# A graph-attention layer on one core: one head's max as relu(A*B - 1) on ScalarE into a PSUM bank, and the units' one-hots on ScalarE

## Chip, cores and metric
The kernel runs on one core of a Trainium2 chip. Its time is the device time of one launch in microseconds (us).

## The reference, cut to what matters
The layer has 6250 nodes with 128 features and 100000 edges, sorted by destination, which crowd at the low node numbers.

```python
e = concatenate([h[src], h[dst]], axis=1)
a_k = exp(relu(e @ W_att_k + b_att_k))                      # k = 1, 2, 3: one value for an edge
att_k = segment_sum(a_k, dst)
avg_a = (a1 / att1[dst] + a2 / att2[dst] + a3 / att3[dst]) / 3
m = avg_a * relu(relu(relu(h[src] @ W1 + b1) @ W2 + b2) @ W3 + b3)
h_neigh = segment_sum(m, dst) / maximum(deg, 1)
out = relu(concatenate([h, h_neigh], axis=1) @ W_c1 + b_c1) @ W_c2 + b_c2
return layernorm(x + out)
```

The exponent splits in two: the logit of an edge is q(dst) + p(src), so exp(relu(q + p)) = max(exp(q) * exp(p), 1).

## The kernel before, in words
**First stage.** TensorE, ScalarE and VectorE compute every node's message row and source logits and store them as `message_table` (131 numbers for each node). After it comes the edge pass, which takes nearly all of the time.

**The edge pass.** Edges come in groups of 256 (two tiles of 128). A *unit* is 4 groups while the unit's number is below 22 and 2 groups from there; there are 120 units. For each tile GpSimd issues one indirect DMA at L1423 (a *gather*) that fetches 128 message rows by source into a ring of 12 slots (`gath` in `work`, four tiles to a slot); for the next unit it must wait until the unit 12 slots back has been summed (`s_sum`). The gather takes its 128 row numbers from the SBUF tensor `src_t`. In each *step* i of the pass, in program order:

- VectorE: `logits_of(i + 1)` (L2051 from the query products in PSUM, L2057 adds the gathered source logits, so it waits for the rows), `weights(i + 1)` (L2077, L2082), `one_hot(i + 3)` (L2009: compares 48 rows of 512 destination numbers with the row number, in place), `add_sums(i - 1)` (L2101, one for each group).
- ScalarE: `mask_copy(i + 1)` (L1783), `exps(i + 1)` (L1743).
- TensorE: `add_edges(i)` (L1610, L1616) waits for `weights(i)`, then `edge_q(i + 2)` (L1562), the query products from the one-hots of that unit. They go to a PSUM bank that `q_bank` picks: bank 1 for units under 22, then banks 3 and 1 in turn.
- SyncE issues the loads (`load_near`, `load_q`, `load_block`) some units ahead.

**Hot nodes.** Edges to the first 512 nodes in the first 108 groups are done densely. In steps 0 to 26 their counts are built: for each block b of 128 source nodes (49 blocks) a table `counts` of 128 sources by 512 hot nodes. In steps 28 to 76, one block for each step ("hot step"), with b = i - 28, VectorE makes three tables of weights, one for each head k, in `hot_wt`: max(hot_b, 1 / power) * counts (`hot_weights`, L1957, 128 by 512). `hot_b` is exp(q) of the hot nodes spread over all partitions, `power` is exp(p) of the block's source nodes. ScalarE multiplies the block's 129 columns (ones and message row, `hot_block`) by `power`, once for each head (`scale_rows`, L1722, into `hot_scaled`). A step later TensorE multiplies the two (`hot_edges`, L1652, 24 matmuls) and adds them up in banks 4 to 7. The three heads have places of their own in a step: k = 0 before `logits_of(i + 1)`, k = 1 after `weights(i + 1)`, k = 2 after `one_hot(i + 3)`.

**Last stage.** The output of 4 blocks at a time (the finals: L966 to L1212) is mixed into the later steps, to the last unit and behind it.

Order is written out by hand; the engines meet at semaphores alone. `counts`, `hot_b`, `hot_wt` (the name `acc` in the profile) and the near rows (`side`) are in SBUF.

## Time and profile before

| what | value |
|---|---|
| median of 3 runs | 797.84 us (796.34 to 806.46) |
| the profiled execution | 793.08 us |
| its span, first to last instruction | 788.9 us |
| around the span | 4.2 us |
| step 28 begins on VectorE (first L1957) | 327.4 us |
| last L1957 | 557.6 us |
| last gather begins | 763.3 us |

Times within the span are counted from its start. The profile shows one execution; its own time is 4.8 us under the median. A row's number of us is one instruction's duration, or that of several merged ones where it ends in x2 or more; the row of the next instruction may start before the one ahead of it has ended, since they overlap in the engine's pipeline. "idle before" in brackets tells how long the engine had nothing to do and who ended that.

### The profile page before, as it was taken

Reading aid. Unit: us, or ns where it says so; the run is one execution under the profiler, and the core shown is the slowest. Engines: PE = TensorE matmul, PEld = TensorE weight load, DVE = VectorE, ACT = ScalarE, POOL = GpSimd, SP = SyncE. Lnnn points to the kernel's source line nnn. Section 1 sums busy time; section 2 is a strip of 40 time slices with the busy share of each in tenths; the row PEclk is TensorE's granted clock in tenths of the full one; section 3 lists DMA queues with packets and bytes.
Section 4 is the critical chain, followed back from the end, with each engine's and each line's share of the span. In section 5 each row is a group of like instructions: output and inputs, shape, how many; then the busy total and the mean of one; then the engine's idle time right before and its main releaser. Section 6 shows DMA issues by size and latency. Waiting matters only on the chain.

```text
span 788.9 us, 17382 instructions
## 1 busy us (share of the span) xinstructions
PE 652.3 (83%) x5388; PEld 533.0 (68%) x5388; DVE 619.5 (79%) x1972; ACT 343.6 (44%) x942; POOL 577.0 (73%) x576
## 2 busy tenths in 40 slices
PE   9962688897987777699999999988787877878775
PEld 5742476665755533489999999877676766767664
DVE  4883588898888878878888888777566888888886
ACT  5554788967745444223333233222232234332433
POOL 7677777777777775577777777777777777777750
PEclk9985599979779575599999999999979899899798
DMA  7974353335843232233333333332432454444431
GB/s 221 257 197 105 67 94 86 85 76 72 83 80 76 63 101 52 57 69 73 75 74 77 72 73 72 75 71 62 129 68 63 104 132 104 116 131 104 113 75 34
DMA packets 81571, 73.69 MB, mean 93 GB/s; under 512 B 34056, under 2 KB 65472, under 8 KB 81472
## 3 DMA queue, kind: packets, MB, share of 16 engines
q0 software_dynamic: 18112, 37.94, 24.1%
q1 hardware_dynamic: 63072, 34.43, 16.4%
q8 instruction: 46, 0.75, 0.4%
q14 instruction: 53, 0.43, 0.2%
q10 hardware_dynamic: 288, 0.13, 0.1%
HBM read 62.91 MB, written 9.52 MB: 92 GB/s over the span
## 4 chain that ended last, share of the span: by engine, by line
PE 35%; POOL 24%; DVE 16%; issue 12%; ACT 6%; DMA 4%; DVEq 2%; SPq 1%; ACTq 0%
POOL work L1423 22%; PE bank L1652 13%; PE bank L1610 7%; DVE counts L1918 4%; PE bank L1636 3%; DVE acc L1903 3%; PE bank L1616 2%; DVE acc L2101 2%; ACT acc L1757 2%; ACT counts L1814 1%; PE bank L1562 1%; ACT acc L1762 1%; DVE side L2009 1%; PE bank L643 1%; PE bank L1567 1%
## 5 line engine op out<-in xcount | busy, mean ns | idle before, releaser
L1423 POOL DMA_INDIRECT work<-message_table,src_t x526 | 535.7, 1018 | 172.0 <-issue 157.3
L1610 PE MATMUL bank<-work 128*128 128x144 f32 (+7 forms) x1132 | 174.9, 308 | 43.2 <-DVE acc L2101 43.1
L1610 PEld LDWEIGHTS bank<-work 128*128 128x128 f32 x1132 | 160.3, 217 | 56.3 <-issue 52.9
L1783 ACT COPY work<-bank 128x192 f32<-128x192 f32 (+5 forms) x120 | 36.3, 302 | 328.3 <-DVE work L2051 328.2
L1652 PE MATMUL bank<-shared,acc 128*128 128x129 f32 (+1 forms) x1176 | 144.2, 279 | 0.0
L1652 PEld LDWEIGHTS bank<-shared,acc 128*128 128x128 f32 (+1 forms) x1176 | 135.1, 191 | 2.2
L1957 DVE SCALAR_TENSOR_TENSOR acc<-logits_or_x,per_node,counts 128x512 f32<-128x512 f32 (+1 forms) x147 | 109.0, 742 | 1.2 <-PE bank L1652 1.2
L2101 DVE TENSOR_TENSOR acc<-acc,bank 128x192 f32 (+7 forms) x283 | 85.3, 301 | 26.6 <-issue 4.2
L2082 DVE TENSOR_TENSOR work<-bank,work 128x576 f32<-128x576 f32 (+5 forms) x120 | 83.5, 696 | 12.5
L1636 PE MATMUL bank<-acc 128*128 128x294 bf16 (+3 forms) x240 | 64.2, 401 | 31.0 <-ACT acc L1762 22.9
L1918 DVE TENSOR_TENSOR counts<-counts,bank 128x294 f32 (+3 forms) x120 | 68.9, 574 | 11.9 <-issue 7.5
L1636 PEld LDWEIGHTS bank<-acc 128*128 128x128 bf16 x240 | 22.4, 111 | 70.2 <-ACT acc L1762 38.0
L1757 ACT ACTIVATE acc<-acc 128x128 bf16<-128x128 f16 x216 | 68.2, 387 | 0.0
L1903 DVE TENSOR_SCALAR acc<-acc 128x294 bf16<-128x294 f16 (+3 forms) x216 | 65.8, 350 | 0.0
L1616 PE MATMUL bank<-work 128*4 128x48 f32 (+7 forms) x1132 | 63.1, 206 | 0.0
L1722 ACT ACTIVATE shared<-work,powers 128x129 f32<-128x129 f32 (+1 forms) x147 | 48.0, 390 | 25.7 <-PE bank L1652 21.0
L1616 PEld LDWEIGHTS bank<-work 128*4 128x4 f32 x1132 | 44.7, 90 | 15.5 <-issue 3.6
L1562 PE MATMUL bank<-side 48*128 48x57 bf16 (+7 forms) x566 | 35.9, 186 | 22.9 <-DMA side<-logit_parts 19.6
L2057 DVE TENSOR_TENSOR work<-work 128x12 f32<-128x12 f32 (+1 forms) x120 | 21.1, 176 | 42.0 <-DMA work<-message_table,src_t 31.2
L2009 DVE TENSOR_SCALAR side<-side,less_col 48x512 bf16<-48x512 bf16 (+1 forms) x142 | 50.9, 371 | 0.0
L1562 PEld LDWEIGHTS bank<-side 48*128 48x128 bf16 x566 | 22.8, 96 | 39.4 <-issue 30.9
L2077 DVE TENSOR_SCALAR work<-work 128x12 f32<-128x12 f32 (+1 forms) x120 | 24.2, 202 | 27.2 <-ACT work L1743 25.8
(180 smaller groups left out, 829.0 us busy)
## 6 DMA issues: line engine op xcount, KB each, us to landing
work<-message_table,src_t POOLq DMA_INDIRECT x526
side<-near_nodes SPq DMA_DIRECT2D x97, 48.0 KB
side<-logit_parts SPq DMA_DIRECT2D x283, 0.8 KB
message_table<-work SPq DMA_DIRECT2D x12, 262.0 KB, 4.1
work<-message_table SPq DMA_DIRECT2D x48, 65.5 KB
work<-in_x_t SPq DMA_DIRECT2D x12, 256.0 KB, 5.5
counts<-in_x SPq DMA_DIRECT2D x11, 256.0 KB, 3.2
logits_or_x<-in_x_t SPq DMA_DIRECT2D x11, 256.0 KB
```

Of the source, the lines that this page charges most:

```text
L1423: pool.indirect_dma_start(out=rows_of(n)[:, t, :], out_offset=None, in_=table[:, :], in_offset=bass.IndirectOffsetOnAxis(ap=src_t[:, h, g: ...
L1562: last = pe.matmul(from_q(i)[:, t, :], near_of(i)[:, t * P:(t + 1) * P], q_eye[:, slot(i, t // TILES), 0:PARTS + width(i)], start=t == 0 i ...
L1610: pe.matmul(sums[:, at:at + HEADS * w], rows_here[:, t, 0:P], wt_of(i)[:, t, :], start=h == 0, stop=h == TILES - 1)
L1616: last = pe.matmul(sums[SUMS_AT:SUMS_AT + HEADS + 1, at + HEADS * w:at + HEADS * w + w], a_col[:, i % THREE, t, :], mask_of(i)[:, t, :], s ...
L1636: pe.matmul(bank[COUNT_BANKS[item % FOUR]][:, 0:(end - begin) * w], hot_lo[:, t % HOT_RING, :], hot_comb(t)[:, begin * w:end * w], start=h ...
L1652: last = pe.matmul(bank[HOT_BANKS[h]][:, k * (P + 1):(k + 1) * (P + 1)], hot_wt[0:m, b % THREE, k, h * P:(h + 1) * P], hot_scaled[0:m, b % ...
L1757: act.activation(hot_lo[:, t % HOT_RING, :], iota16[:, 0:P], ACT.Abs, bias=lo_t[:, g, h:h + 1], scale=-1.0).then_inc(s_lod, 1)
L1903: dve.tensor_scalar(hot_comb(t)[:, 0:n], iota16[:, 0:n], comb_t[:, g, h:h + 1], None, ALU.is_equal).then_inc(s_oh, 1)
L1918: dve.tensor_tensor(here, here, bank[COUNT_BANKS[item % FOUR]][:, 0:w * (end - begin)].rearrange("p (b d) -> p b d", d=w), ALU.add).then_i ...
L1957: dve.scalar_tensor_tensor(hot_wt[0:m, b % THREE, k, :], hot_b[0:m, k, :], inverse[0:m, b, k:k + 1], counts[0:m, b, :], ALU.max, ALU.mult) ...
L2082: dve.tensor_tensor(wt_of(i).rearrange("p t (k w) -> p t k w", w=w), from_q(i)[:, :, PARTS:PARTS + w].unsqueeze(2).to_broadcast([P, n, HEA ...
L2101: dve.tensor_tensor(here, here, sums[:, at:at + (HEADS + 1) * w].rearrange("p (k w) -> p k w", w=w), ALU.add).then_inc(s_acc, 1)
```

## The change
The change has two parts.

**Head 0 of a hot block.** ScalarE computes relu(hot_b * power - 1) of 128 by 512 from SBUF into PSUM bank 3 (`excess(b)`, at the end of ScalarE's step i for b = i - 27). VectorE adds `ok_col` (1 when all exponents are in reach) and multiplies by `counts`: max(A*B, 1) * counts. Since `power` now is in the weight, the rows of head 0 aren't scaled: `scale_rows` is left with k = 1 and 2, and TensorE reads head 0's rows from `hot_block`. Bank 3 is no longer one of the two banks of query products until step 80 (`q_bank`). SyncE's `load_block` now waits for TensorE to have used the block four back.

**One-hots.** From unit 27 on, one-hots are made by ScalarE as relu(1 - |x - row|), two instructions for a unit, instead of one on VectorE (`by_dve`; the ScalarE code for it was there).

```diff
             def q_bank(i):
-                return Q_BANKS[0] if i < n_long else Q_BANKS[i % TWO]
+                return Q_BANKS[0] if first and i < hot_end + 2 else Q_BANKS[i % TWO]
...
             def by_dve(i):
-                return first
+                return first and i < HOT_AT
...
                     def load_block(b):
                         if b >= BLOCKS:
-                            sp.wait_ge(s_hr, HEADS * (b - BLOCKS + 1))
+                            sp.wait_ge(s_hm, b - BLOCKS + 1)
...
-                        pe.wait_ge(s_hr, HEADS * (b + 1))
+                        pe.wait_ge(s_hb[b % BLOCKS], 16 * (b // BLOCKS + 1))
                         for k in range(HEADS):
                             pe.wait_ge(s_hw, HEADS * b + k + 1)
+                            if k >= 1:
+                                pe.wait_ge(s_hr, (HEADS - 1) * b + k)
+                            rows_here = hot_scaled[0:m, b % TWO, k, :] if k >= 1 else hot_block[0:m, b % BLOCKS, 0:1 + P]
...
-                        for k in range(HEADS):
+                        for k in range(1, HEADS):
                             act.activation(hot_scaled[0:m, b % TWO, k, :], hot_block[0:m, b % BLOCKS, 0:1 + P], ACT.Copy,
                                            scale=powers[0:m, b, k:k + 1]).then_inc(s_hr, 1)
+
+                    def excess(b):
+
+                        m = block_nodes(b)
+                        if b == 0:
+                            act.wait_ge(s_hl, 16 * (HEADS * HOT + 1))
+                            act.wait_ge(s_ok, OK_STEPS)
+                            act.wait_ge(s_erow, EARLY)
+                        else:
+                            act.wait_ge(s_hw, HEADS * (b - 1) + 1)
+                        act.activation(bank[EXCESS_BANK][0:m, 0:hot_nodes], hot_b[0:m, 0, :], ACT.Relu, bias=less_one[0:m, 0:1],
+                                       scale=powers[0:m, b, 0:1]).then_inc(s_hx, 1)
...
                             scale_rows(i - HOT_AT - 1)
+                        if first and 0 <= i - HOT_AT < n_blocks:
+                            excess(i - HOT_AT)
...
+                        if k == 0:
+                            dve.wait_ge(s_hx, b + 1)
+                            dve.scalar_tensor_tensor(hot_wt[0:m, b % THREE, k, :], bank[EXCESS_BANK][0:m, 0:hot_nodes],
+                                                     ok_col[0:m, 0:1], counts[0:m, b, :], ALU.add, ALU.mult).then_inc(s_hw, 1)
+                            return
                         dve.scalar_tensor_tensor(hot_wt[0:m, b % THREE, k, :], hot_b[0:m, k, :], inverse[0:m, b, k:k + 1],
                                                  counts[0:m, b, :], ALU.max, ALU.mult).then_inc(s_hw, 1)
```

On VectorE a hot step before: head 0, the logits and weights of unit i + 1, head 1, the one-hots of unit i + 3, head 2:

```order
L1957 SCALAR_TENSOR_TENSOR acc<-logits_or_x,per_node,counts 128x512 [waits s_hm]
L2051 TENSOR_REDUCE work<-bank3 128x12 [waits s_q]
L2057 TENSOR_TENSOR work<-work 128x12 [waits s_qs,s_gath3]
L2077 TENSOR_SCALAR work<-work 128x4x3 [waits s_sum,s_exp]
L2082 TENSOR_TENSOR work<-bank3,work 128x432 [waits s_a,s_mcopy]
L1957 SCALAR_TENSOR_TENSOR acc<-logits_or_x,per_node,counts 128x512 [waits s_hm]
L2009 TENSOR_SCALAR side<-side,less_col 48x512 [waits s_near5]
L1957 SCALAR_TENSOR_TENSOR acc<-logits_or_x,per_node,counts 128x512 [waits s_hm]
```

and a hot step of VectorE now (L1981 is head 0, L1984 heads 1 and 2):

```order
L1981 SCALAR_TENSOR_TENSOR acc<-bank3,ok_col,counts 128x512 [waits s_hx,s_hm]
L2078 TENSOR_REDUCE work<-bank1 128x12 [waits s_q]
L2084 TENSOR_TENSOR work<-work 128x12 [waits s_qs,s_gath1]
L2104 TENSOR_SCALAR work<-work 128x4x3 [waits s_sum,s_exp]
L2109 TENSOR_TENSOR work<-bank1,work 128x432 [waits s_a,s_mcopy]
L1984 SCALAR_TENSOR_TENSOR acc<-logits_or_x,per_node,counts 128x512 [waits s_hm] x2
```

Head 0 has one input in PSUM and a wait on ScalarE (`s_hx`); the one-hots between heads 1 and 2 are gone, so these two now follow each other.

On ScalarE a hot step before:

```order
L1783 COPY work<-bank1 128x128 [waits s_sum,s_qs]
L1743 ACTIVATE work<-work 128x12 [waits s_a,s_lg]
L1722 ACTIVATE shared<-work,powers 128x129 [waits s_hm,s_hb2]
L1722 ACTIVATE shared<-work,powers 128x129 x2
```

and now, where L1753 and L1755 are the one-hots and L1742 is `excess`:

```order
L1803 COPY work<-bank1 128x128 [waits s_sum,s_qs]
L1763 ACTIVATE work<-work 128x12 [waits s_a,s_lg]
L1753 ACTIVATE side<-side,less_col 48x512 [waits s_near2]
L1755 ACTIVATE side<-side,one_col 48x512 [waits s_gap]
L1730 ACTIVATE shared<-work,powers 128x129 [waits s_hm,s_hb3]
L1730 ACTIVATE shared<-work,powers 128x129
L1742 ACTIVATE bank3<-logits_or_x,less_one,powers 128x512 [waits s_hw]
```

Two one-hots and `excess` have come, one of three row scalings has gone, and `excess` stands last in the step. ScalarE's wait for `s_hm` was there before, at the first row scaling; now `excess`, for which VectorE's head 0 waits, is behind it.

## Rows read from the trace of the kernel before

**Rows 1.** The page, first part: busy time, share of the span, instructions
```profile
span 788.9 us, 17382 instructions
...
PE 652.3 (83%) x5388; PEld 533.0 (68%) x5388; DVE 619.5 (79%) x1972; ACT 343.6 (44%) x942; POOL 577.0 (73%) x576
```

**Rows 2.** The chain of waits by line, of 345 to 450, 560 to 715 and 715 to 789
```profile
by line: PE bank L1652 67.0%; PE bank L1610 20.5%; PE bank L1616 8.0%; PE bank L1562 4.6%
...
by line: POOL work L1423 76.2%; issue 24.2%
...
by line: issue 14.4%; PE bank L1013 7.3%; DVE counts L1167 6.2%; DVE acc L2101 6.1%; DVE stats L1188 5.4%; DVE counts L1128 4.7%; DMA work<-message_table,src_t 4.6%; DVE counts L1184 4.4%; DVE side L2009 4.1%; PE bank L1610 4.0%; DVE work L
```

**Rows 3.** Costliest groups of instructions: count | busy us, mean ns | idle before, releaser
```profile
L1423 POOL DMA_INDIRECT work<-message_table,src_t x526 | 535.7, 1018 | 172.0 <-issue 157.3 <-PE bank L1616 14.0 <-DMA message_table<-work 0.4
...
L1957 DVE SCALAR_TENSOR_TENSOR acc<-logits_or_x,per_node,counts 128x512 f32<-128x512 f32 (+1 forms) x147 | 109.0, 742 | 1.2 <-PE bank L1652 1.2
...
L2009 DVE TENSOR_SCALAR side<-side,less_col 48x512 bf16<-48x512 bf16 (+1 forms) x142 | 50.9, 371 | 0.0
...
L1722 ACT ACTIVATE shared<-work,powers 128x129 f32<-128x129 f32 (+1 forms) x147 | 48.0, 390 | 25.7 <-PE bank L1652 21.0 <-issue 4.7
...
L1762 ACT ACTIVATE acc<-acc,one_col 128x512 bf16<-128x512 bf16 x54 | 39.0, 722 | 1.8
```

**Rows 4.** Windows, gathers alone (L1423): us, busy (count), granted clock, DMA
```profile
250.00:300.00 50.00, 37.97 (x40) 0.70 0.32 76
...
560.00:600.00 40.00, 30.23 (x33) 0.87 0.41 99
...
347.20:503.50 156.30, 124.30 (x106) 1.00 0.33 74
```

**Rows 5.** The timeline, one hot step: start us, us, engine, line
```profile
441.86 0.66 DVE L2082 TENSOR_TENSOR work<-bank,work 128x480 f32<-128x480 f32 x1
...
442.43 0.74 DVE L1957 SCALAR_TENSOR_TENSOR acc<-logits_or_x,per_node,counts 128x512 f32<-128x512 f32 x1
443.09 0.34 DVE L2009 TENSOR_SCALAR side<-side,less_col 48x512 bf16<-48x512 bf16 x1
443.29 1.62 POOL L1423 DMA_INDIRECT work<-message_table,src_t  x1 [0.30 <-issue]
443.36 0.73 DVE L1957 SCALAR_TENSOR_TENSOR acc<-logits_or_x,per_node,counts 128x512 f32<-128x512 f32 x1
...
444.69 0.75 DVE L1957 SCALAR_TENSOR_TENSOR acc<-logits_or_x,per_node,counts 128x512 f32<-128x512 f32 x1
...
445.85 0.21 ACT L1743 ACTIVATE work<-work 128x12 f32<-128x12 f32 x1
```

**Rows 6.** The chain of waits in order of time, hot_edges of two steps
```profile
343.36 2.88 PE bank L1652 x24
...
424.96 2.88 PE bank L1652 x24
```

**Rows 7.** The timeline, a gather that waits for a ring slot
```profile
316.82 1.05 POOL L1423 DMA_INDIRECT work<-message_table,src_t  x1 [4.17 <-PE bank L1616]
```

**Rows 8.** The timeline, a late hot step, where units wait for rows
```profile
530.01 0.73 DVE L1957 SCALAR_TENSOR_TENSOR acc<-logits_or_x,per_node,counts 128x512 f32<-128x512 f32 x1
...
530.28 1.28 POOL L1423 DMA_INDIRECT work<-message_table,src_t  x1 [0.30 <-issue]
...
535.73 1.28 POOL L1423 DMA_INDIRECT work<-message_table,src_t  x1 [0.31 <-issue]
```

**Rows 9.** Lines L1174 and L1184: count, duration ns min/median/max, first and last
```profile
L1174 DVE TENSOR_TENSOR counts<-counts,row_b x11: 680/684/685, 608.2 to 759.6; 128x512 f32<-128x512 f32 x11
...
L1184 DVE TENSOR_TENSOR counts<-bank,counts x11: 683/684/692, 613.7 to 763.5; 128x512 f32<-128x512 f32 x11
```

**Rows 10.** The last stage: one-hots in the chain; ScalarE between two steps
```profile
725.97 0.58 DVE side L2009
...
734.57 0.32 ACT L1783 COPY work<-bank 128x192 f32<-128x192 f32 x1 [0.92 <-DVE work L2051]
```

More of the change, by code:

```diff
@@ L235, in gnn_program @@
         one_col = sb("one_col", [P, 1])
+        less_one = sb("less_one", [P, 1])
         eps_col = sb("eps_col", [P, 1])
@@ L534, in _ @@
                 dve.memset(one_col[:, :], 1.0)
+                dve.memset(less_one[:, :], -1.0)
+                dve.memset(shared[:, COLS:5 * P], 0.0)
                 dve.memset(eps_col[:, :], EPS / DOWN)
@@ L693, in gnn_program @@
         HOT_BANKS = SIDE_BANKS + (EXP_BANK,)
+        EXCESS_BANK = Q_BANKS[1]
         assert len(HOT_BANKS) == HOT and (HEADS + 1) * P <= 512
@@ L830, in gnn_program @@
         s_hr = sem("s_hr")
+        s_hx = sem("s_hx")
         s_bound = sem("s_bound")
@@ L1653, in hot_edges @@
                                                  hot_wt[0:m, b % THREE, k, h * P:(h + 1) * P],
-                                                 hot_scaled[0:m, b % TWO, k, :],
+                                                 rows_here,
                                                  start=False, stop=b == n_blocks - 1 and k == HEADS - 1)
```

## Prediction

> **What bounds the kernel now.** I read the page's first part first: no engine is busy all the time, so shares alone decide nothing [rows 1]. The chain of waits, taken stretch by stretch, tells three regimes [rows 2]. From 345 to 450 us it is all TensorE (hot_edges, add_edges). From 560 to 715 us it is the gathers alone (L1423 and the idle time between them, called issue). From 715 us to the end it is a mix with VectorE ahead, in which the one-hots (L2009) hold 4.1% of 74 us, 3.0 us. Then the gathers: 526 of mean 1.018 us, each behind 0.30 us of idle time; only 14.0 us of their waits are for a ring slot [rows 3]. GpSimd issues them to 764 us with hardly a pause, so what shortens or lengthens gathers moves the stretch up to 715 us one for one, as long as the ring isn't full.
>
> A gather takes 37.97 / 40 = 0.95 us before the hot steps and, in 560 to 600 us, 30.23 / 33 = 0.92 (edges of the window cut it); with 0.30 us that is 1.25 us each, 40 in 50 us. In the hot steps the mean is 124.30 / 106 = 1.17 us [rows 4]. The timeline shows why [rows 5]: the gather of 443.29 takes 1.62 us. The L1957 of head 2 (443.36, 0.73) begins just behind its start and ends at 444.09. Of the 1.62 us some 0.67 are waiting, if it is held from 0.13 us behind its start (443.42) to 444.09, and 0.95 are left, the free gather's time. So a gather whose first reading falls into an L1957 waits to that instruction's end. Over the run this costs 526 x (1.018 - 0.949) = 36 us. L1957 reads two tensors in SBUF (`hot_b`, `counts`), the gather its row numbers. The Trainium skill, "SBUF — State Buffer", section "Who interferes with whom", says the same: a VectorE instruction with two SBUF inputs contends with a GpSimd instruction that reads SBUF, and one with a single SBUF input outside the two-port modes does not. By that rule head 0, now read from PSUM, no longer holds up a gather; no row of an L1957 with PSUM input exists here.
>
> This is a rhythm, not a scatter. The window from head 0 of block 4 (347.20) to head 0 of block 39 (503.50), 35 steps, holds 106 gathers: 3 for each step, of 4.47 us [rows 4]. 3 free gathers would take 3.75 us; the fourth would need a start in the stretch that heads 1 and 2 cover, is thrown behind head 2, and the round begins again. A unit needs 4 gathers, so the ring is used up in these steps, and from block 39 on the units wait for rows.
>
> **The change part by part.**
>
> *VectorE in a hot step.* The one-hots go: from 443.09 to 443.36, 0.27 us of the step [rows 5]. Head 0 stays one instruction of 512 columns, from PSUM. Nearest rows for the price of that: L1174 (both inputs in SBUF) and L1184 (one in PSUM) both take 684 ns [rows 9], so 0; bounds -0.06 and +0.10 us. The Trainium skill, "VectorE: DVE Perf Modes", section "The TRN2 errata", gives 120 cycles of fixed cost from PSUM against 58 from SBUF, by which head 0 would be 0.065 us longer; rows 9 speak against it, and the sum would lose some 49 x 0.065 = 3 us at most, were VectorE the bound. VectorE's round, 4.47 us in the mean of the 35 steps and near 4.5 at the timeline's, goes to 4.20 and near 4.25 us.
>
> *ScalarE in a hot step.* From the start of head 0 (444.69) to the end of the exponentials (446.06) are 1.37 us [rows 5]. Then come in order, by the nearest rows: two one-hot instructions of 512 columns, 0.72 each (L1762, 128 by 512 bf16), two row scalings, 0.39 each with some overlap, 0.65, and `excess`, 0.72 as well, bounds 0.39 (L1722, 129 columns) and 1.0 [rows 3]. Sum 1.37 + 1.44 + 0.65 + 0.72 = 4.18 us, after which VectorE's next head 0 may start. Behind `excess` nobody but head 0 waits; behind a late head 0 all of VectorE's step. `excess` also stands behind the row scalings' old wait for hot_edges two blocks back, so VectorE can lead TensorE by less; that costs nothing while TensorE sets the pace.
>
> *TensorE.* The work is the same: 24 + 8 + 8 + 4 matmuls. Between block 0's and block 19's hot_edges, 343.36 to 424.96, a step takes 81.60 / 19 = 4.295 us [rows 6], some 4.35 at 40 columns. The new wait is that of edge_q(i + 2) for weights(i + 1), since bank 3 is taken; hot_edges of the step are queued behind it, and they feed nobody urgent. The weights end some 2.4 us after head 0 starts (1.37 to the exponentials, 1.0 for L2077 and L2082, 0.66 of it in L2082's row [rows 5]), and TensorE comes back to edge_q every 4.3 us: over 1 us to spare. I cost it at 0. Behind step 80 the banks alternate as before.
>
> *So the step becomes 4.30 to 4.35 us, TensorE's*, since VectorE's 4.25 and ScalarE's 4.18 are under it. With heads 1 and 2 now back to back (1.40 us) the rhythm of 3 gathers for a step holds up to a step of about 1.26 + 3 x 1.25 - 0.60 = 4.41 us (1.26: head 2's end less 0.13; a gather that comes in the last 0.06 of head 1 or later is thrown behind head 2). So 3 gathers a step stay, but the steps are shorter: 20 x 4.30 + 15 x 4.35 = 151.3 us against 156.3. **Gain 5.0 us**; bounds 0 (the step stays) and see the rival.
>
> *Late hot steps, blocks 39 to 48.* Here 4 gathers make a unit. The gather of 530.28 is held by head 2 (530.01 to 530.74): 1.28 us, 0.33 too long, and the one behind it by head 0, 0.12; the unit takes 535.73 - 530.28 = 5.45 us, where 4 x 1.25 = 5.0 [rows 8]. After, head 0 holds nobody, head 2 ends 0.27 to 0.34 us sooner, and about 0.1 us is left. Gain 0.35 to 0.40 for each of 10 units, **3.8 us**; bounds 0 and 5.
>
> *Steps 24 to 27.* The ring is full there and gathers wait for TensorE [rows 7], which waits for VectorE's add_sums behind the one-hots: 4 x 0.27 = **1.1 us** gained. ScalarE's 1.44 us come in idle time ahead of L1783. The start of block 3, where head 0 now waits for hot_edges plus scalings plus excess (0.65 + 0.72 more), costs **0.5 us** of VectorE's lead.
>
> *560 to 715 us.* The gathers set the pace at 1.25; a few of them no longer meet L2009. **0.5 us** gained. ScalarE's one-hots lie in its slack.
>
> *715 us on.* The 8 one-hots in the chain, 0.33 to 0.58 us (725.97: 0.58), 3.0 us by the share, go [rows 2, 10]. Against this, one-hots end a ScalarE step, and where its finals are long only 0.92 us are idle before L1783 [rows 10], less than 1.44: exps come 0.5 us late, in one or two of these steps. **Net 2.4 us**; bounds -1 and 3.
>
> *SyncE.* load_block now waits for hot_edges four blocks back, with near rows and query parts of later steps queued behind it; they are issued six and more steps ahead, at least 20 us, the block itself three steps. 0. Two more memsets in the first stage: under 0.2 us off the path, 0.
>
> Sum: 5.0 + 3.8 + 1.1 - 0.5 + 0.5 + 2.4 = 12.3 us. From the profiled 793.08 that gives 780.8. The median of the runs is 4.8 us above that execution, so the forecast for the median is 797.84 - 12.3 = 785.5 us, 1.5% less. What a measurement of this kernel can tell from no change is about 2%, 16 us.
>
> **Rivals.**
>
> *The rhythm breaks, and gathers run nearly free.* If a step gets longer than the 4.41 us above (ScalarE's sum is only 0.23 under it, and width grows), the gather slips past head 2 in every other step: 3.5 for a step, 0.5 x 1.25 = 0.6 us gained each. For it: 0.06 us decides. Against: TensorE's 4.30 in most steps. Over 15 to 38 steps 9 to 24 us are gained by the gathers; units behind the hot steps must then catch up, with VectorE busy for 79% of the time as it is [rows 1], so half of it may count. Time 785.5 - 4 to 785.5 - 16, 770 to 781.
>
> *Contention stays.* Heads 1 and 2 back to back are as long a barrier as all three were; late steps shift phase and the gather falls into head 1. Then only steps 24 to 27 and the end are left, 3 us, less with late exponentials: 791 to 799.
>
> *Slower: ScalarE becomes the bound of the hot steps.* Its chain head 0, exps, one-hots, scalings, excess closes on the next head 0. If a 512-column instruction costs more than the row says or its waits cost 0.2 us each, the step grows. From 5.0 us (four gathers) gathers are free and the hot steps bind: at 5.6 us 49 x (5.6 - 4.7) = 44 us are lost (4.7: 327.4 to 557.6 us over 49 steps), of which the 42 later units, which had 5.0 and by VectorE's share could do 4.6, win back 17. That is 797.84 + 27 - 2 = 823. It decides from about 5.0. Against: the four 512-column or scaling steps behind the exponentials would have to take 1.4 us more than the rows say for 5.6.
>
> **How the numbers follow.** Forecast (781 to 791) 0.50; rhythm breaks 0.20; contention stays 0.22; slower 0.08. The range that leaves out about 2 in 10 is 773 to 799. Faster by over 2% (under 781.9): the rival's 0.20 and the forecast's lower edge 0.08, 0.28. Slower by over 2% (over 813.8): 0.05. Within: 0.67.
>
> **What would show it.** Head 0 and one-hots: L1981 at 0.74 and no L2009-like row after step 24. Hot steps: head 0 every 4.30 to 4.35 us; a window of 35 steps with 105 gathers; if it holds over 115, the first rival. Late hot steps: 5.1 us a unit. Last head-0 instruction near 547 us instead of 557. `excess` and one-hots near 0.7 us. VectorE idle before L1981 by ScalarE for over 0.3 us a step would speak for the slower rival; idle TensorE before edge_q would show the bank to cost. The chain from 560 us still of gathers. The prediction is wrong if gathers meet head 0 in PSUM as before, or if exps late behind the one-hots show in 560 to 715 us.

## The result, and the profile after

The changed kernel takes 772.43 us (median of 4 runs, 770.84 to 774.35); the kernel before took 799.41 us beside it (4 runs). The ratio is 0.965, with a 95% interval of 0.958 to 0.972: faster by 27 us, where 12.3 us and a time of 785.5 us were predicted. Medians are of all runs and ratios of the fast runs alone, since some executions come out 1 to 2% slower, so a ratio can differ from the quotient of the two medians. The time lies 0.6 us under the low end of the range, 773. The profiled execution took 772.04 us, 21.0 us less than that of before (793.08).

The page of the changed kernel, first part, and the costliest groups that answer to [rows 1] and [rows 3]:

```profile
span 767.9 us, 17623 instructions
...
PE 651.9 (85%) x5388; PEld 535.7 (70%) x5388; DVE 593.9 (77%) x1881; ACT 486.6 (63%) x1128; POOL 553.2 (72%) x576
...
L1428 POOL DMA_INDIRECT work<-message_table,src_t x526 | 511.8, 973 | 178.4 <-issue 155.9
...
L1755 ACT ACTIVATE side<-side,one_col 48x512 bf16<-48x512 bf16 (+1 forms) x93 | 66.9, 720 | 3.0
...
L1753 ACT ACTIVATE side<-side,less_col 48x512 bf16<-48x512 bf16 (+1 forms) x93 | 65.7, 707 | 0.0
```

The gathers (now L1428) are busy for 511.8 us instead of 535.7: the same 526 of them, 23.9 us less, where the two executions differ by 21.0 us. The new one-hots on ScalarE cost 0.71 and 0.72 us each. Head 0 is a line of its own now (count: duration ns min/median/max, first and last start; then what VectorE idled for before it):

```profile
L1981 DVE SCALAR_TENSOR_TENSOR acc<-bank,ok_col,counts x49: 744/751/753, 331.8 to 542.8; 128x512 f32<-128x512 f32 x48, 106x512 f32<-106x512 f32 x1
...
  ACT bank L1742: 4.0, 1
```

The chain of waits by line, of 345 to 450, 450 to 545 and 560 to 715 us:

```profile
by line: PE bank L1660 67.2%; PE bank L1615 20.3%; PE bank L1621 8.0%; PE bank L1567 4.6%
...
by line: PE bank L1660 42.4%; POOL work L1428 26.5%; PE bank L1615 13.8%; issue 8.5%; PE bank L1621 6.1%; PE bank L1567 3.0%
...
by line: POOL work L1428 64.5%; issue 22.9%; DMA work<-message_table,src_t 2.4%; ACT counts L1100 2.0%; ACT counts L1050 1.3%; DVE acc L2128 0.8%; ACT counts L1058 0.7%; DVE counts L1133 0.7%; DVEq L1407 0.6%; DVE stats L1193 0.6%; DVE coun
```

The first stretch is TensorE's and the last the gathers', as in [rows 2]; from 450 to 545 us, in the late hot steps, the gathers already hold 26.5%. The windows of the gathers, as in [rows 4]: before the hot steps, behind them, from head 0 of block 4 to head 0 of block 39, and from there to the last head 0:

```profile
250.00:300.00 50.00, 36.45 (x39) 0.72 0.32 75
560.00:600.00 40.00, 30.27 (x32) 0.86 0.36 82
352.38:503.42 151.04, 116.27 (x115) 1.00 0.35 80
...
503.42:542.85 39.43, 29.98 (x32) 1.00 0.36 81
```

A free gather costs what it did (30.27 / 32 = 0.95 us). The 35 steps of the third window take 151.04 us, 4.315 each; predicted were 151.3. But they hold 115 gathers where 105 were predicted, 116.27 / 115 = 1.01 us each instead of 1.17 [rows 4]. So rows are there when the late hot steps come: these take (542.85 - 503.42) / 9 = 4.38 us each, not the 5.45 of [rows 8], and from 495 to 564 us VectorE never waits for a gather's rows, where it did so 10 times before, for 11.3 us.

Where the time comes from is seen by laying the start of each unit's first logits instruction (L2051 before, L2078 after) side by side, in us from the two spans' starts:

```
unit          24     33     66     81    117    end
before     287.9  347.9  495.1  579.6  760.2  788.9
after      294.1  353.0  495.4  563.6  740.8  767.9
after less  +6.2   +5.2   +0.3  -16.0  -19.4  -21.0
before
```

From unit 24 on 27.2 us are gained: 1.0 to unit 33, 4.9 to unit 66, **16.3 from unit 66 to 81**, and 5.0 behind them. Of the 16.3, 12.1 fall up to unit 78, where the late hot steps end, and 4.2 in the three units behind them. Up to unit 24 the changed kernel loses 6.2 us.

### The profile page after: what moved, and what is told of

It reads as the page before. It is cut to its first block, busy times and chain, and to the rows that moved or that the text cites. A ratio compares the mean times of both kernels' runs of the same rounds, so it can differ in the third digit from the quotient of the medians.

```text
span 767.9 us, 17623 instructions
## 1 busy us (share of the span) xinstructions
PE 651.9 (85%) x5388; PEld 535.7 (70%) x5388; DVE 593.9 (77%) x1881; ACT 486.6 (63%) x1128; POOL 553.2 (72%) x576
## 4 chain that ended last, share of the span: by engine, by line
PE 43%; POOL 22%; DVE 13%; issue 12%; ACT 6%; DMA 2%; DVEq 1%; SPq 0%; ACTq 0%
POOL work L1428 22%; PE bank L1660 15%; PE bank L1615 9%; PE bank L1641 3%; PE bank L1621 3%; DVE counts L1940 3%; DVE acc L1925 2%; DVE acc L2128 2%; ACT acc L1777 2%; PE bank L646 2%; PE bank L667 2%; PE bank L1567 1%; DMA work<-message_table,src_t 1%; PE bank L655 1%; PE bank L1572 1%
## 5 line engine op out<-in xcount | busy, mean ns | idle before, releaser
L1428 POOL DMA_INDIRECT work<-message_table,src_t x526 | 511.8, 973 | 178.4 <-issue 155.9
L1615 PE MATMUL bank<-work 128*128 128x144 f32 (+7 forms) x1132 | 175.8, 310 | 24.0 <-DVE acc L2128 23.9
L1615 PEld LDWEIGHTS bank<-work 128*128 128x128 f32 x1132 | 163.6, 220 | 33.8 <-issue 19.3
L1660 PE MATMUL bank<-shared,acc 128*128 128x129 f32 (+1 forms) x784 | 95.6, 275 | 0.0
L2109 DVE TENSOR_TENSOR work<-bank,work 128x576 f32<-128x576 f32 (+5 forms) x120 | 83.5, 696 | 12.5
L1660 PEld LDWEIGHTS bank<-shared,acc 128*128 128x128 f32 (+1 forms) x784 | 91.5, 192 | 0.0
L1984 DVE SCALAR_TENSOR_TENSOR acc<-logits_or_x,per_node,counts 128x512 f32<-128x512 f32 (+1 forms) x98 | 69.4, 749 | 0.0
L1755 ACT ACTIVATE side<-side,one_col 48x512 bf16<-48x512 bf16 (+1 forms) x93 | 66.9, 720 | 3.0
L1753 ACT ACTIVATE side<-side,less_col 48x512 bf16<-48x512 bf16 (+1 forms) x93 | 65.7, 707 | 0.0
L1660 PE MATMUL bank<-work,acc 128*128 128x129 f32 (+1 forms) x392 | 56.7, 288 | 0.0
L1660 PEld LDWEIGHTS bank<-work,acc 128*128 128x128 f32 (+1 forms) x392 | 47.5, 191 | 2.2 <-issue 0.2
```

What stands on the lines that cost most here:

```text
L1428: pool.indirect_dma_start(out=rows_of(n)[:, t, :], out_offset=None, in_=table[:, :], in_offset=bass.IndirectOffsetOnAxis(ap=src_t[:, h, g: ...
L1615: pe.matmul(sums[:, at:at + HEADS * w], rows_here[:, t, 0:P], wt_of(i)[:, t, :], start=h == 0, stop=h == TILES - 1)
L1660: last = pe.matmul(bank[HOT_BANKS[h]][:, k * (P + 1):(k + 1) * (P + 1)], hot_wt[0:m, b % THREE, k, h * P:(h + 1) * P], rows_here, start=Fa ...
L1755: act.activation(here, here, ACT.Relu, bias=one_col[0:WIN, 0:1], scale=-1.0).then_inc(s_hot, 1)
L1984: dve.scalar_tensor_tensor(hot_wt[0:m, b % THREE, k, :], hot_b[0:m, k, :], inverse[0:m, b, k:k + 1], counts[0:m, b, :], ALU.max, ALU.mult) ...
L2109: dve.tensor_tensor(wt_of(i).rearrange("p t (k w) -> p t k w", w=w), from_q(i)[:, :, PARTS:PARTS + w].unsqueeze(2).to_broadcast([P, n, HEA ...
```

## The experiments

Four of the five sets of runs fell on chips where the kernel before takes 984 to 1004 us, and no kernel's time moves there by much. What they show is in their traces; times on a chip where the gathers bound the kernel exist for the changed kernel and for the lighter pair only.

**The parts one by one.** The first set, on a chip where the kernel before took 985.28 us (31 runs). The excess alone: the changed kernel, with the first one-hots on VectorE throughout.

```
 def by_dve(i):
-    return first and i < HOT_AT
+    return first
```

> The changed kernel with every unit's one-hots back on VectorE; head 0 stays as relu(A*B - 1) in PSUM. Theory P (port): the gain comes from gathers that no longer meet head 0's two SBUF inputs, so over half of the 27 us stays: 776 to 788 us, more than 3.0 gathers for a hot step, hot step 4.35 to 4.5 us. Theory V (VectorE's share): the gain comes from a VectorE step that got 0.27 us shorter, so nearly all is lost: 793 to 800 us with 3.0 gathers for a hot step.

983.66 us, ratio 0.999 (0.995 to 1.003).

The one-hots alone: the kernel before, with that line the other way round.

```
 def by_dve(i):
-    return first
+    return first and i < HOT_AT
```

> The kernel before with only the one-hots from unit 27 on moved to ScalarE; head 0 as before, from SBUF. Theory P: head 0, head 1 and head 2 all hold gathers up, the step shortens to about 4.3 us, 3.0 gathers a step stay: 785 to 793 us. Theory V: VectorE's step is as short as in the changed kernel, so nearly all of the gain is here: 772 to 778 us.

988.44 us, ratio 1.002 (0.999 to 1.004).

The changed kernel with its excess in SBUF, so that head 0 has two SBUF inputs again:

```
+excess_sb = acc[:, HEADS, KEPT + 600:KEPT + 600 + hot_nodes]
...
-act.activation(bank[EXCESS_BANK][0:m, 0:hot_nodes], hot_b[0:m, 0, :], ...
+act.activation(excess_sb[0:m, :], hot_b[0:m, 0, :], ...
...
-dve.scalar_tensor_tensor(hot_wt[0:m, b % THREE, k, :], bank[EXCESS_BANK][0:m, 0:hot_nodes],
+dve.scalar_tensor_tensor(hot_wt[0:m, b % THREE, k, :], excess_sb[0:m, :],
```

> The changed kernel with relu(A*B - 1) written to SBUF instead of PSUM bank 3; the same instructions on every engine, but VectorE's head 0 has two SBUF inputs again. Theory P: gathers meet head 0 again, 3.0 gathers for a hot step, late hot steps wait for rows: 783 to 793 us. Theory V: the same time as the changed kernel, 770 to 775 us.

987.04 us, ratio 0.995 (0.991 to 0.999).

The changed kernel with head 2 moved behind the two sums, so that heads 1 and 2 no longer touch:

```
-if hot_step:
-    hot_weights(i - HOT_AT - 1, 2)
...
 if i >= 1:
     add_sums(i - 1)
+if hot_step:
+    hot_weights(i - HOT_AT - 1, 2)
```

> The changed kernel with head 2 of the hot weights moved behind the step's add_sums, so that heads 1 and 2 stand some 0.8 us apart on VectorE instead of back to back. Theory P with a rhythm: each head can hold a gather for 0.6 us at most and two may be held in one round, the rate stays between 3.2 and 3.5 gathers a hot step: 766 to 776 us. If back to back heads were one barrier, apart gives 3.4 or more and 766 us; theory V: no difference, 771 to 774 us.

987.64 us, ratio 1.002 (0.998 to 1.005). No time here tells anything apart, so the set was repeated with the changed kernel as a yardstick, on a second chip (before 983.75 us):

> The changed kernel once more, as the yardstick for the runs beside it. On a chip where the kernel before takes some 797 us: 770 to 775 us. On a chip as in the first set of experiments, where the kernel before takes 985 us: the gathers aren't the bound there, so within 1% of the kernel before.

985.17 us, ratio 1.000 (0.995 to 1.005): the change gains nothing on such a chip.

> The changed kernel with every unit's one-hots back on VectorE, repeated because the first set ran where the kernel before takes 985 us and showed nothing of the gain. Theory P (port): over half of the 27 us stays, 776 to 788 us, more than 3.0 gathers for a hot step. Theory V (VectorE's share): 793 to 800 us, 3.0 gathers for a hot step.

982.24 us, 0.999 (0.994 to 1.003).

> The kernel before with only the one-hots from unit 27 on moved to ScalarE, repeated. Theory P: three heads hold gathers up, step near 4.3 us, 3.0 gathers a step: 785 to 793 us. Theory V: 772 to 778 us.

986.49 us, 1.004 (0.999 to 1.008).

> The changed kernel with relu(A*B - 1) in SBUF instead of PSUM, repeated. Theory P: 3.0 gathers for a hot step again, 783 to 793 us. Theory V: as the changed kernel, 770 to 775 us.

982.78 us, 0.999 (0.995 to 1.003). A third chip (before 984.55 us):

> The changed kernel once more, as the measure for its parts. Two conditions are possible, told apart by the time of the kernel before on the same chip. If that is near 797 us, gathers bound the kernel, both theories expect 0.96 to 0.97 of it (about 772), and the hot steps from 360 to 520 us hold 10 gathers in three steps at a granted clock near 1.00. If it is near 984 us, TensorE stands still between its own instructions in the hot steps, its clock there is near 0.9, VectorE and GpSimd have idle time in every step, and both theories expect a ratio of 0.995 to 1.005.

985.3 us, 0.998 (0.994 to 1.002).

> The changed kernel with every first one-hot back on VectorE; only the excess in PSUM is left of the change. Theory P (the gathers are freed because head 0 no longer reads SBUF with two inputs): most of the gain stays, 772 to 783 us where the kernel before takes 797, and at least 3.2 gathers to a hot step. Theory V (the gathers are freed because VectorE has a short instruction less in front of the heads and its step is shorter): the gain is mostly lost, 788 to 798 us, and a gather that waits behind heads 1 and 2. Where the kernel before takes 984 us both expect no difference (0.995 to 1.005).

981.4 us, 0.995 (0.991 to 0.999).

> The kernel before with the first one-hots of units from the second stage on moved to ScalarE as in the change, all three heads as before from SBUF. Theory P: 788 to 798 us where the kernel before takes 797, three gathers to a hot step. Theory V: 773 to 785 us, more than three gathers to a hot step. Where the kernel before takes 984 us both expect no difference.

988.27 us, 1.005 (1.001 to 1.009).

> The changed kernel with the excess of head 0 written by ScalarE into SBUF instead of PSUM, so that VectorE's three heads all have two SBUF inputs; nothing else differs. Theory P: head 0 holds gathers again, some 5 us of waiting in its row, and with it the time goes to 780 to 795 us where the kernel before takes 797. Theory V: within 0.5% of the changed kernel (770 to 777). Where the kernel before takes 984 us both expect no difference in time, and theory P still expects the gathers' sum to be 5 to 8 us above the changed kernel's.

979.64 us, 0.993 (0.989 to 0.997).

**What these traces do show: who holds a gather.** In the changed kernel 29 gathers begin so that a head 0 in PSUM covers the point 0.13 us behind their start. All took 0.94 to 0.95 us, as free ones do; so did 182 such gathers in the seven other traces with head 0 in PSUM and heads 1 and 2 in their places (up to 0.96 us). One of them, in the timeline of the changed kernel:

```profile
369.45 0.75 DVE L1981 SCALAR_TENSOR_TENSOR acc<-bank,ok_col,counts 128x512 f32<-128x512 f32 x1
369.96 0.95 POOL L1428 DMA_INDIRECT work<-message_table,src_t  x1 [0.30 <-issue]
```

The same head with its excess in SBUF (the second run of that kernel) holds one to its end, 468.84, and 0.82 us later the gather is done:

```profile
468.09 0.75 DVE L1983 SCALAR_TENSOR_TENSOR acc<-acc,ok_col,counts 128x512 f32<-128x512 f32 x1 [0.31 <-ACT acc L1744]
468.26 1.40 POOL L1430 DMA_INDIRECT work<-message_table,src_t  x1 [0.30 <-issue]
```

Over the run this shows in the gathers' busy time, the cleanest yardstick on these chips (us for 526 gathers, all runs of each kernel):

```
changed                       516.8  517.5
excess in SBUF                522.9  524.9  522.6  524.3
excess alone (e1)             524.5  523.6  524.8  519.8
one-hots alone (e2)           519.5  521.8  516.6  518.6
heads 1 and 2 apart (e5)      511.4  511.9
```

The excess in SBUF costs 5 to 8 us of gather time, as theory P said. The rule of the Trainium skill that the prediction named ("SBUF — State Buffer", section "Who interferes with whom"), by which a VectorE instruction with two SBUF inputs contends with a GpSimd instruction that reads SBUF and one with a single SBUF input doesn't, agrees with both timelines: 0.95 us against 1.40. The excess alone leaves more holding than the one-hots alone, 523.2 against 519.1 us in the mean: theory P, by which head 0 was to bring most of it, gets no support from that.

**The lighter pair.** To see whether TensorE hides the effect on such chips, 4 of the 12 hot matmuls of each block but the last (the profile counts two for each) were left out in both kernels, so that their sums over hot nodes are incomplete.

```
-for h in range(HOT):
+for h in range(TWO if 1 <= k and b < n_blocks - 1 else HOT):
     last = pe.matmul(bank[HOT_BANKS[h]][:, k * (P + 1)...
...
```

> The kernel before, with 4 of the 12 hot matmuls of every block but the last left out (heads 1 and 2 of the last two banks), so the sums over hot nodes are incomplete; nothing else differs, and TensorE has about 0.98 us less to do in a hot step at its full clock. It is the base of the lighter pair. On a chip where the kernel before takes 984 us: theory S (TensorE's own pauses and the lower clock after them make TensorE the bound of the hot steps there, and this hides what the change does for gathers) expects 930 to 955 us; theory N (what is slow there slows every engine's work alike) expects 970 to 984 us.

> The changed kernel with the same 4 of 12 hot matmuls left out, against the lighter kernel before of the same call. Theory S expects the change to gain again once TensorE has room, 10 to 25 us below the lighter kernel before, with more gathers to a hot step and fewer that wait than in it. Theory N expects the two within 0.5% of each other. If the kernel before takes 797 us on the chip, the changed one should again lead by 20 to 30 us, in the light form too, since VectorE and the gathers and not TensorE set the time there.

The chip was one on which the kernel before takes 800.91 us, so the question of the slow chips stayed, and a better one was answered. The lighter kernel before: 799.42 us, ratio 0.999 (0.995 to 1.002). The lighter changed one: 783.99 us, ratio 0.978 (0.973 to 0.984); both ratios are to the whole kernel before. It was expected 20 to 30 us ahead and is 15 to 17; **with less work for TensorE the changed kernel is 11.6 us slower** than whole. The two times weren't taken side by side, but the kernel before took 799.41 us beside the one and 800.91 beside the other, and the intervals of the ratios, 0.973 to 0.984 here and 0.958 to 0.972 for the whole change, don't meet. The windows of the gathers tell why. First the lighter kernel before, from head 0 of block 4 to that of block 39:

```profile
350.69:506.89 156.20, 124.19 (x106) 1.00 0.33 74
```

This is [rows 4] to 0.1 us: with a third of the hot matmuls gone the step didn't change. The chain of waits had given that stretch to TensorE, L1652 with 67% [rows 2]; in the lighter kernel it is VectorE's, and just as long. So VectorE set the step of the kernel before: its own was 4.47 us, while hot_edges followed each other every 4.295 [rows 6], since TensorE was still catching up. Then the lighter changed kernel, 20 steps and 35:

```profile
353.73:436.93 83.20, 64.91 (x61) 1.00 0.36 79
353.73:500.80 147.07, 114.76 (x107) 1.00 0.36 78
```

Its steps are shorter than the whole kernel's, 83.20 / 20 = 4.16 us, later up to 4.26, 4.20 in the mean, as VectorE's share was predicted. And it has exactly 3 gathers to a step there, 60 in 20 (the window counts one that reaches in); in all 35 steps only one, of 4.33 us, has 4. Two of its steps in the timeline:

```profile
409.87 1.40 DVE L1984 SCALAR_TENSOR_TENSOR acc<-logits_or_x,per_node,counts 128x512 f32<-128x512 f32 x2
410.72 1.37 POOL L1428 DMA_INDIRECT work<-message_table,src_t  x1 [0.30 <-issue]
...
412.40 0.94 POOL L1428 DMA_INDIRECT work<-message_table,src_t  x1 [0.30 <-issue]
413.64 0.94 POOL L1428 DMA_INDIRECT work<-message_table,src_t  x1 [0.30 <-issue]
414.05 1.40 DVE L1984 SCALAR_TENSOR_TENSOR acc<-logits_or_x,per_node,counts 128x512 f32<-128x512 f32 x2
414.89 1.38 POOL L1428 DMA_INDIRECT work<-message_table,src_t  x1 [0.30 <-issue]
```

This is the rhythm that the prediction described: every third gather begins 0.84 to 0.85 us behind head 1 (head 2 begins 0.66 behind it), is held to the end of head 2, and the round begins again. (After the one step with 4 gathers, from 469 us on, it is head 1 that holds every third gather: it begins 0.10 us behind head 1's start and takes 1.45 us, again with 3 to a step.) Now three steps of the whole changed kernel, 4.30 us each, set by TensorE:

```profile
414.68 1.45 DVE L1984 SCALAR_TENSOR_TENSOR acc<-logits_or_x,per_node,counts 128x512 f32<-128x512 f32 x2
415.41 0.95 POOL L1428 DMA_INDIRECT work<-message_table,src_t  x1 [0.30 <-issue]
416.66 0.95 POOL L1428 DMA_INDIRECT work<-message_table,src_t  x1 [0.31 <-issue]
417.91 0.95 POOL L1428 DMA_INDIRECT work<-message_table,src_t  x1 [0.30 <-issue]
418.98 1.40 DVE L1984 SCALAR_TENSOR_TENSOR acc<-logits_or_x,per_node,counts 128x512 f32<-128x512 f32 x2
419.16 1.38 POOL L1428 DMA_INDIRECT work<-message_table,src_t  x1 [0.30 <-issue]
420.85 0.94 POOL L1428 DMA_INDIRECT work<-message_table,src_t  x1 [0.30 <-issue]
422.10 0.94 POOL L1428 DMA_INDIRECT work<-message_table,src_t  x1 [0.30 <-issue]
423.29 1.45 DVE L1984 SCALAR_TENSOR_TENSOR acc<-logits_or_x,per_node,counts 128x512 f32<-128x512 f32 x2
423.34 0.96 POOL L1428 DMA_INDIRECT work<-message_table,src_t  x1 [0.30 <-issue]
...
427.11 0.95 POOL L1428 DMA_INDIRECT work<-message_table,src_t  x1 [0.30 <-issue]
427.59 1.40 DVE L1984 SCALAR_TENSOR_TENSOR acc<-logits_or_x,per_node,counts 128x512 f32<-128x512 f32 x2
428.36 1.45 POOL L1428 DMA_INDIRECT work<-message_table,src_t  x1 [0.30 <-issue]
```

Ten gathers begin from 415.41 to 427.11, in three steps (two of them are left out above). The one that begins 0.73 us behind head 1 (415.41) is free, though head 2 has begun 0.07 us before. The one of 428.36, 0.77 behind head 1, is held for 0.5 us. The one of 419.16 begins in head 1 and gets through at head 1's end, for 0.43 us of waiting, though head 2 has begun. The one of 423.34, 0.05 behind head 1's start, is free. So a gather gets past head 2 if it begins up to 0.73 us behind head 1, and not at 0.77.

**A last try at the parts**, with the rhythm in view. It fell on a chip where the kernel before took 1003.92 us.

> The changed kernel with every first one-hot back on VectorE, so of the change the excess in PSUM is left. Theory P (head 0 from PSUM holds no gather, so a gather is held by heads 1 and 2 alone, and a hot step of over 4.30 us lets a fourth gather in now and then, where the lighter changed kernel at 4.17 to 4.26 us had exactly three): over 3.2 gathers to a hot step and 772 to 783 us where the kernel before takes 797 to 801. Theory V (a shorter step of VectorE is what frees the gathers): three gathers to a hot step and 790 to 800 us. If the kernel before takes 984 us, nothing shows.

1000.02 us, ratio 0.999 (0.995 to 1.003).

> The kernel before with its first one-hots from the second stage on made by ScalarE; all three heads as before from SBUF. Theory P: three heads in a row still hold a gather, the rhythm of exactly three to a step stays, late blocks take over 5 us, and the time is 786 to 797 us (a shorter step alone gives the 5 us of the steps before block 39). Theory V: more than three gathers to a step and 772 to 783 us.

1002.33 us, ratio 1.001 (0.996 to 1.005).

> The changed kernel with the excess of head 0 in SBUF instead of PSUM, nothing else. Theory P: head 0 holds gathers again (some 5 us of waiting in its row at least), and with it the rhythm of three comes back in part or whole: 778 to 795 us. Theory V: within 0.5% of the changed kernel, 769 to 777 us.

1000.08 us, ratio 0.997 (0.993 to 1.001).

> The changed kernel with head 2 of each hot step moved behind the two sums that follow heads 1 and 2, so that no two operations with two SBUF inputs of 0.74 us stand in a row. Theory P: a waiting gather is held by one head only, the gathers' sum falls by some 5 us below the changed kernel's 512 us, and the time is 768 to 776 us, unless TensorE, which waits for head 2, ends 0.7 us later in each step; then 795 us or more. Theory V expects nothing from it but the later head 2: 790 to 810 us.

997.72 us, ratio 0.992 (0.988 to 0.996).

Two places in these traces show what the one-hot between the heads does. With the excess alone it is there (L2036), and head 2 begins 0.92 us behind head 1 instead of 0.66. A gather that begins 0.74 us behind head 1 by these rows (0.746 unrounded) is held from the one-hot on to the end of head 2, 506.48, and takes 1.74 us:

```profile
504.82 0.74 DVE L1984 SCALAR_TENSOR_TENSOR acc<-logits_or_x,per_node,counts 128x512 f32<-128x512 f32 x1
505.48 0.34 DVE L2036 TENSOR_SCALAR side<-side,less_col 48x512 bf16<-48x512 bf16 x1
505.56 1.74 POOL L1428 DMA_INDIRECT work<-message_table,src_t  x1 [0.30 <-issue]
505.74 0.74 DVE L1984 SCALAR_TENSOR_TENSOR acc<-logits_or_x,per_node,counts 128x512 f32<-128x512 f32 x1
```

With the one-hots alone moved, a gather that begins 0.71 us behind head 1 is free:

```profile
514.07 1.44 DVE L1957 SCALAR_TENSOR_TENSOR acc<-logits_or_x,per_node,counts 128x512 f32<-128x512 f32 x2
514.78 0.94 POOL L1423 DMA_INDIRECT work<-message_table,src_t  x1 [0.30 <-issue]
```

So the gate, the latest start with which a gather still gets past head 2, stands at the same place with the one-hot and without. All kept traces with heads 1 and 2 in these places agree: no gather that begins 0.60 to 0.73 us behind head 1 takes over 0.97 us, and none that begins 0.75 to 0.93 behind it takes under 1.29, in either form. The gate is near 0.74 us. What the one-hot moves is the end of head 2, from 1.40 to 1.66 us behind head 1.

Heads apart holds gathers for less in both of its runs, by 5 to 6 us (511.4 and 511.9 against 516.8 and 517.5), the amount that theory P gave. That it is 0.8% faster here and 0.2% slower in the first set leaves its worth open, and on a chip where gathers bound the kernel it wasn't run.

## Why the prediction was wrong

**The step that failed** is the limit of the rhythm, "3 gathers for a step holds up to a step of about 1.26 + 3 x 1.25 - 0.60 = 4.41 us". The form of it is right: the lighter changed kernel keeps 3 to a step for block after block. The 0.60 is the term that was mis-sized. It put the last start with which a gather gets past head 2 at 0.06 us before head 2's own (0.66 behind head 1); the runs show that it may begin up to 0.07 us after that, 0.73 behind head 1 (free), and not at 0.77 (held), with the gate near 0.74. So the limit is 1.26 + 3.75 - 0.74 = 4.27 us. The lighter changed kernel's steps, 4.09 to 4.26, lie under it and hold 3 gathers. In the whole changed kernel the steps of blocks 4 to 8 take 4.26 to 4.27 us and hold 3 each; of those that follow, of 4.30 to 4.31 us, every fourth holds a fourth gather, and of those of 4.34 from block 26 on every third, 115 in 35 steps. The prediction put its steps, 4.30 to 4.35, rightly, and on the wrong side of the limit.

**What the change did** is then another thing than the prediction summed. In the kernel before, a round looks like this (heads 1 and 2 at 465.03 and 465.95, then the next head 0):

```profile
465.03 0.74 DVE L1957 SCALAR_TENSOR_TENSOR acc<-logits_or_x,per_node,counts 128x512 f32<-128x512 f32 x1
465.89 1.62 POOL L1423 DMA_INDIRECT work<-message_table,src_t  x1 [0.31 <-issue]
465.95 0.74 DVE L1957 SCALAR_TENSOR_TENSOR acc<-logits_or_x,per_node,counts 128x512 f32<-128x512 f32 x1
467.28 0.75 DVE L1957 SCALAR_TENSOR_TENSOR acc<-logits_or_x,per_node,counts 128x512 f32<-128x512 f32 x1
467.81 1.04 POOL L1423 DMA_INDIRECT work<-message_table,src_t  x1 [0.30 <-issue]
469.15 0.95 POOL L1423 DMA_INDIRECT work<-message_table,src_t  x1 [0.30 <-issue]
470.40 1.62 POOL L1423 DMA_INDIRECT work<-message_table,src_t  x1 [0.30 <-issue]
```

Head 2 holds one gather, and head 0 the next for another 0.1 us (1.04). The third after the held one begins 470.40 - 465.03 = 5.37 us behind head 1; with the gate at 0.74 it is held again in every step under 4.63 us, and the steps from block 4 to 39 were 4.35 to 4.59. Both parts of the change lower that limit. Without the one-hot between the heads, head 2 ends 0.26 us sooner (1.40 instead of 1.66 behind head 1), and with head 0 in PSUM the 0.1 us go: from 4.63 to 4.27, while the step fell only from 4.47 to 4.315. The kernel before sat inside the rhythm, the changed one outside it. That is the first rival, "the rhythm breaks, and gathers run nearly free", with its 770 to 781 us, by another way than it named: it looked for a longer step, and its 3.5 gathers for a step are 3.3.

Term by term, profiled against profiled:

- *Head 0 from PSUM, bounds -0.06 and +0.10 us*: 0.750 us in the mean, where head 0 had 0.746 from SBUF. The 0.065 us more that the Trainium skill gives ("VectorE: DVE Perf Modes", section "The TRN2 errata") would make 0.81 of it; no row shows that. The gathers that meet it are free.
- *One-hots on ScalarE at 0.72, excess never waited for*: 0.707 and 0.720; VectorE waited for the excess once in the run, for 4.0 us, at block 3. The slower rival is out.
- *Hot steps before block 39, 5.0 us*: 4.9, from unit 33 to 66. TensorE set the step, as forecast; the extra gathers of these steps pay only later.
- *Steps 24 to 27 and block 3, 1.1 - 0.5 us*: 1.0 to unit 33, which is 1.6 gained up to unit 28 and 0.6 lost behind it. The wait at block 3 is 4.0 us where VectorE waited 1.2 before; the shorter steps around it pay most of that back.
- *Late hot steps, 3.8 us*: 16.3, from unit 66 to 81. This is by far the largest error. With 10 gathers more by block 39 no unit waits for its rows, and a step is 4.38 us. In the lighter pair, where the changed kernel kept the rhythm as well, the same stretch gave 4.9 us (from -5.6 at unit 66 to -10.5 at 81) and the steps before it 8.6.
- *560 us on, 0.5 + 2.4 us*: 5.0, from unit 81 on, 3.4 of it up to unit 117. This late gain isn't explained one by one.
- *Not in the sum at all*: up to unit 24 the changed kernel is 6.2 us later. The lighter pair shows 6.1 at the same unit, so this is likely no accident of one execution. In both pairs the logits are 3.5 to 3.7 us later by unit 7, while in the whole pair the gathers begin within 0.8 us of where they did up to 280 us. Of the change only the two memsets and the bank of the query products from unit 22 on stand there, and no run was made for it. It is open.

The sum closes: against the terms the changes of -0.1, +0.4, +12.5, +2.1 and -6.2 us make 8.7, and the profiled execution is 780.8 - 772.04 = 8.8 us under the forecast for it. The median of the kernel before was 6.3 us above its profiled execution and that of the changed kernel 0.4, which makes the rest of the 27 us.

What stays open too: how much of the gain is due to head 0 in PSUM and how much to the one-hots. An estimate from the rows above speaks against crediting either alone. With the excess alone, the step is VectorE's, 4.35 to 4.52 us as before and once 4.59, and the limit is 1.52 + 3.75 - 0.74 = 4.53, so the rhythm would have held for most of the stretch. With the one-hots alone, the step is TensorE's, 4.30 to 4.35; the gather behind the held one begins 2.53 us behind head 1, a head 0 in SBUF ends there at 2.80 to 2.85 and holds it for 0.14 to 0.19 us (until 0.82 us behind its own end), which puts the limit at 4.41 to 4.46, over the step again. Only both together bring the limit clearly under the step. That is argued from the traces; no run shows it in time where gathers bound the kernel.

## What to carry to other kernels

When a queue of equal operations of one engine is blocked by a periodic operation of another, look for a locked ratio before costing anything: count both over a long window (106 gathers, 35 steps), and work out the step lengths between which the ratio holds. A forecast that lies within 0.1 us of such a limit, as here, deserves an even chance on either side. And the chain of waits can give a stretch to an engine that is only catching up, while another sets the step: a third of TensorE's hot matmuls taken out left the time of the kernel before where it was, and in the changed kernel it made things worse.

## What the hardware showed that was not expected

*Less work, more time.* 784.0 against 772.4 us, for the reason above: the shorter step falls back into the rhythm of 3 gathers.

*Chips differ by a quarter.* Four sets of runs fell on chips where the kernel before takes 984 to 1004 us instead of 797 to 801. Windows of TensorE (us, busy, granted clock), first of the changed kernel on the faster kind of chip, then of its third run, on a slower one:

```profile
500.00:540.00 40.00, 40.00 (x403) 1.00 0.36 81
```

```profile
500.00:540.00 40.00, 35.57 (x290) 0.87 0.30 66
```

290 matmuls instead of 403 in 40 us of hot steps. The timeline of the slower chip shows pauses of TensorE, of 0.2 to 0.4 us and one of 1.2 from 500 to 522 us, that nothing explains in the records (the one of 1.2 is put down to a one-hot of ScalarE that had ended 0.8 us before), and behind them slower matmuls:

```profile
507.57 1.95 PE L1660 MATMUL bank<-shared,acc 128*128 128x129 f32 x16
...
515.00 0.37 PE L1660 MATMUL bank<-work,acc 128*128 128x129 f32 x1 [0.32 <-issue]
515.17 3.39 PE L1660 MATMUL bank<-shared,acc 128*128 128x129 f32 x16
```

16 matmuls take 1.95 us in one block and 3.39 in the next; the granted clock was 1.00 over the first 16 and 0.56 over the second, most of them at 1.2 GHz instead of 2.4. Gathers, heads and one-hots last as long as on the faster chips (the gathers 0.98 us in the mean), but GpSimd waits for ring slots, 88.4 us for add_edges by the waits of that run against 21.3 in the changed kernel on the faster chip. So the gathers aren't the bound there, and a change that speeds them up gains nothing, as sixteen ratios between 0.992 and 1.005 show, two of them of the changed kernel itself. Why TensorE pauses there wasn't found: the lighter pair, meant for it, met a faster chip.
